# Statistics and attention of a macaron block: normed rows from two tensors, both variances in one addition, maxima turned before the projection

## The chip, the cores and the metric

The kernel runs on one core of a Trainium2 chip. Its time is the device time of one execution in microseconds (us); the number compared is the median of several executions.

## The reference

The input is x of 32 x 256 tokens with 128 features, in fp32. Three steps follow one another, each adding to x:

```
x = x + 0.5 * ffn(layernorm(x))
x = x +       attention(layernorm(x))
x = x + 0.5 * ffn(layernorm(x))

layernorm(x) = (x - mean) / sqrt(var + 1e-5)            over the 128 features
attention:  qkv = x @ (s * W_qkv);  16 heads of 8;  causal softmax(q k^T / sqrt(8)) v;  @ (s' * W_proj)
ffn:        8 experts (128 -> 512 -> 128, gelu), one expert per token by its affinity
            aff = num / (|x| |w|),  num = x @ waff^T;  a token is kept if its rank for its expert is under a capacity
```

The capacity and the ranks need the affinities of all tokens, so each ffn has a routing stage before its experts. s and s' come from spectral norms of the weights.

## The kernel before

The program is a list of blocks in which all engines take part, with a barrier between two: `preamble` (weights, constants), `token_stats` (layernorm statistics and affinity products of the input), `route`, `experts`, `attention`, then `route` and `experts` again. Each engine has its own order of instructions, written out by hand, and waits on semaphores.

**token_stats** goes over 16 batches of 4 tiles of 128 tokens. SP loads a batch (256 KB) into one of four buffers once its former content has been stored. VectorE takes `bn_stats` and `bn_aggr` of each tile, which leaves mean and variance beside the row. Two operations (lines 434 and 435) then put the bare variance and the variance plus 1e-5 into `vare`; POOL raises the two to the powers 0.5 and -0.5 (line 393), which gives the reciprocal deviation for the row and the norm for the affinity. ScalarE's queue stores the rows with their statistics. VectorE norms the tiles of the batch before (line 441, one operation for each of four tiles), PE transposes them and multiplies them with the affinity weights.

**attention** goes over the 32 sequences in turns of 12 steps (u = 0 to 11). A turn b works on several sequences at once. PE's order in each step is: one tile of scores by query of a later sequence, whose row maxima VectorE takes (`tensor_reduce`, line 1341); one tile of scores by key of sequence b (`scores_by_key`, lines 1202 to 1216), which ScalarE turns into exponentials (line 1131) and POOL masks (line 1080); in every third step the products with v; and one small piece of other work (`small`, lines 1236 to 1290). Scores by key alternate between two PSUM banks, so those of step u wait for the exponential of step u - 2; those of step 0 also wait for the maxima, which lie in six rows of `qs`.

The maxima of sequence b + 1 go this way: when VectorE has taken all twelve tiles, POOL splits them into three bf16 pieces in step 5 (lines 1108 to 1114, semaphore `mp_done`); PE transposes them in step 8 into PSUM tile mi[0] (line 1288); ScalarE copies them in step 8, behind the exponential of step 8 (line 1168); SP sends them to `qs` (line 1045); and `scores_by_key` of step 0 of the next turn waits for them (line 1206). In the same step 8, ahead of the transposes, PE multiplies the normalised attention output of sequence b - 1 with W_proj into mi[1] (line 1280, semaphore `proj_mm`), which waits for ScalarE's copy `ont`. VectorE adds the residual in step 9 (line 1376), then takes the statistics of the new rows in steps 10 and 11.

Queries and keys of sequence b + 3 are split into bf16 pieces in steps 2 to 5 (lines 1142, 1350, 1151, and 1102 on POOL), stored to DRAM by SP (line 1040) and loaded back in their final layout, by SP (line 1052) and by ScalarE's queue in steps 9 and 10 (line 1177, three DMAs in each, ahead of the exponential of the next step).

Layernorm appears twice in a turn: for sequence b + 4 before attention (statistics in steps 6 and 7 with one variance, normed rows in step 10), and for sequence b - 2 after it (both variances in step 11, normed rows in step 2 of a later turn). Their helpers are `statistics` (lines 1314 to 1321) and `normalise` (lines 1323 to 1326).

Of the kernel before, what the change touches and what calls it, by code (L numbers as in the profile page):

```python
# [14 lines left out]
ALU = mybir.AluOpType  # L15
# [3 lines left out]
P = 128  # L19
D = 128  # L20
# [3 lines left out]
TPB = S // P  # L24
# [13 lines left out]
LN_EPS = 1e-5  # L38
# [54 lines left out]
def preamble(nc, m, io, c):  # L93

    ctx = ExitStack()
    with ctx:
# [155 lines left out]
        def _(dve):  # L252
            v = nc.vector
# [12 lines left out]
            v.memset(gelu_b1[:, :], 0.0).then_inc(filled, 1)  # L266
            v.memset(c.b1t[:, E, :], 0.0).then_inc(filled, 1)
            v.memset(c.cst[:, :, :], 0.0).then_inc(filled, 1)
            dve.wait_ge(ints, 4)
            for dst, src in ((c.iota[:, :], iota_i[:, :]), (c.part[:, :], part_i[:, :]),  # L270
                             (c.tile1[:, :], tile_i[:, :]), (c.down[:, :], down_i[:, :])):
# [61 lines left out]
def token_stats(nc, m, io, c, x_dram):  # L333
# [3 lines left out]
    with ctx:  # L337
        t = Mem(nc, ctx)
        TS = 4
# [81 lines left out]
        @blk.vector  # L421
        def _(dve):
            v = nc.vector

            def stats(b, k):
                q = k % 2
                dve.wait_ge(x_in[k], b * (16 // NX) + (16 - k * (16 // NX)))
                for j in range(TS):
                    v.bn_stats(bn[:, q, j, :], x_row[k][:, j, 0:D]).then_inc(bn_done, 1)
                dve.wait_ge(bn_done, b * TS + TS)  # L430
                for j in range(TS):
                    v.bn_aggr(x_row[k][:, j, D:D + 2], bn[:, q, j, :]).then_inc(mv_done, 1)
                dve.wait_ge(mv_done, b * TS + TS)
                v.tensor_copy(vare[:, q, :, 1], x_row[k][:, :, D + 1])
                v.tensor_scalar(vare[:, q, :, 0], x_row[k][:, :, D + 1], LN_EPS, None, ALU.add).then_inc(var_done, 1)

            def norm(b, k):
                dve.wait_ge(rstd, b + 1)
                wait(dve, tr, (b - 1) * TS)
                for j in range(TS):  # L440
                    v.tensor_scalar(xn[k % 2][:, j, :], x_row[k][:, j, 0:D], x_row[k][:, j, D:D + 1],
                                    x_row[k][:, j, D + 1:D + 2], ALU.subtract, ALU.mult).then_inc(xn_done, 1)

            def step(b, k, first, last):
                if first:
                    stats(b, k)
                if not last:
                    stats(b + 1, (k + 1) % NX)
                norm(b, k)

            run(step)
# [25 lines left out]
def consts(nc, m):  # L477

    class C:
        pass  # L480
    c = C()
    c.ident, c.ones = m.sb("ident", [P, P]), m.sb("ones", [P, P])
    c.identb, c.onesb, c.tri = (m.sb(n, [P, P], BF16) for n in ("identb", "onesb", "tri"))
    c.tie = m.sb("tie", [P, TPB, S])
    c.mask = m.sb("mask", [P, 4, P], BF16)
    c.iota, c.part, c.tile1, c.down = m.sb("iota", [P, P]), m.sb("part", [P, 1]), m.sb("tile1", [P, NT]), m.sb("down", [P, E])
    c.w1, c.w2 = m.sb("w1", [P, G, F]), m.sb("w2", [P, G, FC, D])


    c.b1t = m.sb("b1t", [P, G, FC])  # L490
    c.cst = m.sb("cst", [P, G, D], BF16)
    c.waff_t, c.wnorm, c.thr = m.sb("waff_t", [P, E]), m.sb("wnorm", [P, E]), m.sb("thr", [P, 1])
    c.wq, c.wk, c.wv, c.wproj = (m.sb(n, [P, D]) for n in ("wq", "wk", "wv", "wproj"))
    c.num, c.xnorm = m.sb("num", [P, NT, E]), m.sb("xnorm", [P, NT])
    c.qs = [m.sb(f"qs{k}", [P, HP, S], BF16) for k in range(NQ)]
    c.kb = [m.sb(f"kb{k}", [P, HP, 2, S], BF16) for k in range(NQ)]
    c.vp = [m.sb(f"vp{k}", [P, TPB, H, 32]) for k in range(NQ)]
    c.gidx, c.sidx = m.sb("gidx", [P, NSX], I32), m.sb("sidx", [P, NSX], I32)
    c.eid = m.sb("eid", [1, NSX], I32)
    c.keep = m.sb("keep", [P, NSX])  # L500
    c.const_parts = m.sb("const_parts", [G, 3, D], BF16)
    c.cst_in = m.sem("cst_in")
    c.place = m.sb("place", [P, NT], I32)
    return c
# [436 lines left out]
def attention(nc, m, io, c, x_dram):  # L941
# [9 lines left out]
    with ctx:  # L951
# [229 lines left out]
        def _(pe):  # L1181
            te = nc.tensor

            def turn(b, k, has):
# [51 lines left out]
                def small(u):  # L1236
                    if u == 0 and has(3):
                        wait(pe, xn_done, (b + 4) * TPB)
                        wait(pe, mt_out, b + 1)
                        wait(pe, v_out, b + 3)  # L1240
                        for j in range(TPB):
                            te.transpose(mi[0][:, j * P:(j + 1) * P], xn[(k + 1) % 2][:, j, :], c.ident[:, :]).then_inc(xt_tr, 1)
                    if u == 3 and has(-2):
                        wait(pe, xn2_done, (b - 1) * TPB)
                        for j in range(TPB):
                            te.transpose(mi[1][:, j * P:(j + 1) * P], xn2[k % 2][:, j, :], c.ident[:, :]).then_inc(x2t_tr, 1)
                    if u == 2 and has(3):
                        wait(pe, xt_out, b + 4)
                        te.matmul(mi[0][:, 0:S], c.wq[:, :], xt[(k + 1) % 2][:, :], start=True, stop=True)
                        te.matmul(mi[0][:, S:2 * S], c.wk[:, :], xt[(k + 1) % 2][:, :], start=True, stop=True).then_inc(qk_mm, 1)  # L1250
                    if u == 7 and has(-2):
                        wait(pe, x2t_out, b - 1)
                        wait(pe, v_out, b + 4, B)
                        for j in range(TPB):
                            last = te.matmul(mi[0][:, j * E:(j + 1) * E], x2t[k % 2][:, j * P:(j + 1) * P], c.waff_t[:, :],
                                             start=True, stop=True)
                        last.then_inc(num_mm, 1)
                    if u == 5 and has(3):
                        wait(pe, r_done, b + 4)
                        for j in range(TPB):  # L1260
                            last = te.matmul(mi[0][:, j * D:(j + 1) * D], xt[(k + 1) % 2][:, j * P:(j + 1) * P], c.wv[:, :],
                                             start=True, stop=True)
                        last.then_inc(v_mm, 1)
                    if u == 5 and has(-1):
                        wait(pe, ot_out, b)
                        wait(pe, x2t_out, b - 1)
                        for j in range(TPB):
                            for half in range(2):
                                at = (2 * j + half) * P
                                last = te.transpose(mi[1][:, at:at + P], ot[(k - 1) % 2][:, half, j * P:(j + 1) * P], c.ident[:, :])  # L1270
                        last.then_inc(otr, 1)
                    if u == 7 and has(-1):
                        wait(pe, on_done, b)
                        for j in range(TPB):
                            last = te.transpose(mi[1][:, j * P:(j + 1) * P], on[(k - 1) % 2][:, j, :], c.ident[:, :])
                        last.then_inc(ont_tr, 1)
                    if u == 8 and has(-1):
                        wait(pe, ont_out, b)
                        for j in range(TPB):
                            last = te.matmul(mi[1][:, j * D:(j + 1) * D], ont[(k - 1) % 2][:, j * P:(j + 1) * P], c.wproj[:, :],  # L1280
                                             start=True, stop=True)
                        last.then_inc(proj_mm, 1)
                    if u == 8 and has(1):
                        wait(pe, mp_done, b + 2)
                        wait(pe, v_out, b + 4, B)
                        wait(pe, num_out, b - 1)
                        for j in range(TPB):
                            last = te.transpose(mi[0].bitcast(BF16)[0:3 * H, j * P:(j + 1) * P],
                                                mp[(k + 1) % 2][:, j, :, :].rearrange("p t h -> p (t h)"), c.identb[:, :])
                        last.then_inc(mt_tr, 1)  # L1290

                for u in range(NP):
                    for o, v in QUERY_TILES[u]:
# [13 lines left out]
        def _(dve):  # L1307
# [6 lines left out]
            def statistics(n, x, bns, var, bnd, mv, done, keep):  # L1314
# [2 lines left out]
                    v.bn_aggr(x[:, j, D:D + 2], bns[:, j, :]).then_inc(mv, 1)  # L1317
                wait(dve, mv, n * TPB + TPB)
                if keep:
                    v.tensor_copy(var[:, :, 1], x[:, :, D + 1])  # L1320
                v.tensor_scalar(var[:, :, 0] if keep else var[:, :], x[:, :, D + 1], LN_EPS, None, ALU.add).then_inc(done, 1)

            def normalise(out, x, done):
                for j in range(TPB):
                    v.tensor_scalar(out[:, j, :], x[:, j, 0:D], x[:, j, D:D + 1], x[:, j, D + 1:D + 2],
                                    ALU.subtract, ALU.mult).then_inc(done, 1)

            def turn(b, k, has):
                for u in range(NP):
# [108 lines left out]
```

## Time and profile before

| | |
|---|---|
| median of 3 runs | 1154.74 us (1152.61 to 1157.74) |
| profiled execution | 1151.91 us, span 1149.8 us |
| PE busy | 910.6 us (79%) |
| VectorE (DVE) busy | 707.3 us (62%) |
| ScalarE (ACT) busy | 592.5 us (52%) |
| GpSimd (POOL) busy | 719.7 us (63%) |
| mean granted TensorE clock | 0.877 of full |

A row of the trace names a line of the kernel, the engine, the operation and the tiles (output, arrow, inputs, buffer numbers left out), and its duration. PE is the matmul, PEld the load of its weights, SPq and ACTq are the queues from which DMAs are issued. In brackets stands how long the engine was idle before the row, and by what the profile supposes that the wait was ended. Where an instruction waits for several semaphores, one releaser is named.

The stages by time: preamble to about 44 us, statistics to 93, the first routing to 165, the experts to 327, attention to 883, the second routing to 950, and the experts to the end.

### The profile page before, as it was taken

The numbers are of one execution on the slowest core, as the hardware profiler recorded it, in microseconds if no ns is written. First come the engines' busy times: TensorE is split into PE (matmuls) and PEld (weight loads), VectorE is DVE, ScalarE is ACT, GpSimd is POOL, SyncE is SP. The second block draws the span as 40 slices with busy tenths as digits, with TensorE's granted clock in tenths as the row PEclk, the third lists the DMA queues.
The fourth block names the chain that finished last, engine by engine and source line by source line (L and its number), as shares of the span: only waits on it lengthen the run. The fifth ranks groups of instructions, "written<-read, shape, count | busy, mean of one in ns | idle before, by whom it ended". The sixth has DMA issues, their size and how long they took to land. (4 is left out here: it accounts for less than half of the span.)

```text
span 1149.8 us, 25202 instructions
## 1 busy us (share of the span) xinstructions
PE 910.6 (79%) x8020; PEld 689.5 (60%) x8054; DVE 707.3 (62%) x2090; ACT 592.5 (52%) x1538; POOL 719.7 (63%) x1170
## 2 busy tenths in 40 slices
PE   2484638999936899999999999999883455988876
PEld 1383218999933566566666666666552225977876
DVE  6587944444416677777778777778654973433332
ACT  3023506666612666666666666666562423654543
POOL 4361976444132677777777777777552596777775
PEclk9655558999968999999999999999996556999998
DMA  5370002222216555555555665555510001212121
GB/s 165 88 191 20 1 9 65 69 67 68 51 47 118 104 104 113 118 117 106 111 108 109 122 116 102 112 113 111 106 27 10 1 1 41 52 52 52 48 50 30
DMA packets 124693, 89.01 MB, mean 77 GB/s; under 512 B 13649, under 2 KB 115078, under 8 KB 124566
## 3 DMA queue, kind: packets, MB, share of 16 engines
q1 hardware_dynamic: 101782, 52.36, 20.8%
q0 software_dynamic: 8960, 18.14, 6.9%
q10 hardware_dynamic: 13824, 16.92, 6.9%
q8 instruction: 68, 1.11, 0.4%
q14 instruction: 59, 0.48, 0.2%
HBM read 52.23 MB, written 34.87 MB: 76 GB/s over the span
## 5 line engine op out<-in xcount | busy, mean ns | idle before, releaser
L1341 DVE TENSOR_REDUCE at_mx<-at_pp 128x2 f32<-128x512 f32 (+1 forms) x384 | 260.4, 687 | 85.9 <-PE at_pp L1199 64.7
L1131 ACT ACTIVATE at_pt<-at_pm 128x512 f32<-128x512 f32 x384 | 224.6, 597 | 143.1 <-PE at_pm L1210 92.7
L1080 POOL TENSOR_SCALAR_AFFINE_SELECT at_pt<-at_pt 128x256 f32<-128x256 f32 (+1 forms) x384 | 182.1, 485 | 127.4 <-ACT at_pt L1131 123.1
L845 ACT ACTIVATE e_ht<-e_ps_h,b1t 128x128 f32<-128x128 f32 x576 | 164.5, 371 | 119.4 <-PE e_ps_h L873 119.2
L807 POOL DMA_INDIRECT e_x<-rows,gidx x144 | 138.6, 963 | 95.0 <-DVE e_y L925 49.1
L873 PE MATMUL e_ps_h<-e_xnt,e_w1own 128*128 128x128 f32 x1152 | 157.8, 281 | 25.5 <-issue 22.0
L873 PEld LDWEIGHTS e_ps_h<-e_xnt,e_w1own 128*128 128x128 f32 x1152 | 143.9, 197 | 29.5 <-issue 28.3
L883 PE MATMUL e_ps_y<-w,e_ht 128*128 x1152 | 160.1, 283 | 0.0
L883 PEld LDWEIGHTS e_ps_y<-w,e_ht 128*128 128x128 f32 x1152 | 140.8, 193 | 1.7
L925 DVE SCALAR_TENSOR_TENSOR e_y<-e_ps_y,e_x 128x256 f32<-128x256 f32 x72 | 30.5, 424 | 143.9 <-PE e_ps_y L883 143.9
L574 POOL TENSOR_SCALAR r_atp<-r_iotab,r_colp 128x128 bf16<-128x128 bf16 x128 | 91.5, 733 | 35.9 <-DVE r_colp L712 35.9
L1231 PE MATMUL at_po<-at_pt,vp 128*32 128x256 f32 (+1 forms) x2048 | 109.8, 332 | 0.9 <-POOL at_pt L1080 0.9
L1210 PE MATMUL at_pm<-qs,kb 128*128 128x256 bf16 x512 | 97.5, 271 | 15.4 <-ACT at_pt L1131 13.5
L1197 PE MATMUL at_pp<-kb,qs 96*128 96x512 bf16 x256 | 98.8, 386 | 2.8 <-DVE at_mx L1341 2.0
L817 POOL DMA_INDIRECT out_dram<-e_y,sidx x72 | 73.4, 1019 | 24.4 <-issue 20.9
L1231 PEld LDWEIGHTS at_po<-at_pt,vp 128*32 128x32 f32 x2048 | 53.4, 109 | 49.7 <-issue 17.6
L1210 PEld LDWEIGHTS at_pm<-qs,kb 128*128 128x128 bf16 x512 | 47.2, 97 | 56.4 <-DMA qs<-at_mt 17.7
L1091 POOL DMA_INDIRECT at_xa<-x,at_index x64 | 63.7, 996 | 13.1 <-issue 10.8
L1199 PE MATMUL at_pp<-mask,identb 128*128 128x256 bf16 x256 | 70.3, 274 | 0.0
L919 DVE COPY e_w1own<-w 128x512 f32 x144 | 63.9, 446 | 8.5 <-issue 7.9
L1192 PE MATMUL at_pp<-kb,qs 96*128 96x256 bf16 x256 | 50.3, 278 | 15.2 <-DMA kb<-at_qkd 14.2
L839 ACT ACTIVATE e_xnt<-e_ps_x 128x256 f32<-128x256 f32 x72 | 27.8, 387 | 52.7 <-PE e_ps_x L866 52.7
(256 smaller groups left out, 1622.7 us busy)
## 6 DMA issues: line engine op xcount, KB each, us to landing
at_qkd<-at_part SPq DMA_DIRECT2D x64, 192.0 KB, 3.0
kb<-at_qkd SPq DMA_DIRECT2D x64, 96.0 KB
qs<-at_qkd ACTq DMA_DIRECT2D x64, 96.0 KB
x<-e_y SPq DMA_DIRECT2D x36, 128.0 KB, 1.8
rows<-ts_x ACTq DMA_DIRECT2D x16, 264.0 KB, 3.1
rows<-at_x SPq DMA_DIRECT2D x32, 132.0 KB
ts_x<-in_x_dram SPq DMA_DIRECT2D x16, 256.0 KB, 3.2
x_by_token<-at_xa SPq DMA_DIRECT2D x32, 128.0 KB
```

The source lines that it names most:

```text
L574: last = g.tensor_scalar(at_p[:, n, :], iotab[:, :], colp[:, n:n + 1], None, ALU.is_equal)
L807: pool.indirect_dma_start(x_row[s][:, j % 2, :], None, rows, bass.IndirectOffsetOnAxis(ap=c.gidx[:, j:j + 1], axis=0)).then_inc(x_in[s], 16)
L817: pool.indirect_dma_start(y_dram, bass.IndirectOffsetOnAxis(ap=c.sidx[:, j:j + 1], axis=0), y_row[s][:, j % 2, :], None, bounds_check=T - ...
L845: last = a.activation(hid_t[j % NB][:, f, :], ps_h[j % NB][:, f, :], ACT.Gelu, bias=c.b1t[:, ds(e, 1), f])
L873: last = te.matmul(ps_h[j % NB][:, f, :], w1_own[j % NB][:, f * P:(f + 1) * P], xn_t[(j // 2) % NX][:, j % 2, :], start=True, stop=True, s ...
L883: last = te.matmul(out, hid_t[j % NB][:, f, :], c.w2[:, ds(e, 1), f, :].rearrange("p a d -> p (a d)"), start=False, stop=(f == FC - 1))
L1080: g.affine_select(out=tile, in_=tile, compare_op=ALU.is_ge, fill=0.0, base=0, pattern=[[0, n], [1, P]], channel_multiplier=-1).then_inc(ma ...
L1131: a.activation(pt[u % RING][:, :], pm[u % 2], ACT.Exp, scale=SCALE).then_inc(exped, 1)
L1197: te.matmul(out, qs[s][0:ROWS, v - 4, P:S], kb[s][0:ROWS, v - 4, :, :].rearrange("p r q -> p (r q)"), start=True, stop=False, skip_group_c ...
L1210: last = te.matmul(out[:, i * S:(i + 1) * S], kb[s][:, g + 2 * w + i, r, 0:P], qs[s][:, g + 2 * w + i, :], start=True, stop=True)
L1231: last = te.matmul(out[32 * j:32 * j + 32, (half + 1) * S - cols:(half + 1) * S], values[:, w // 2, at:at + 32], src[:, i * cols:(i + 1) * ...
L1341: v.tensor_reduce(out, src, axis=AX.X, op=ALU.max).then_inc(maxed, 1)
```

## The change

1. Normed rows, in `token_stats` and in attention's `normalise`: (x - mean) * r was one `tensor_scalar` with two per-partition scalars. It becomes one `scalar_tensor_tensor` with the mean as per-partition scalar and r as a tensor that is one element wide and broadcast over 128.
2. Both variances, in `token_stats` and in `statistics` with `keep`: a `tensor_copy` and a `tensor_scalar` become one `tensor_tensor` addition of the variance, broadcast over two, and a small table `eps` that holds 1e-5 and 0. The single variance becomes a `tensor_tensor` addition with the same table. The table is filled by two `memset`s in the preamble.
3. PE in step 8 of attention: the two transposes of the maxima stand ahead of the projection matmuls, with their waits.

```diff
@@ preamble, VectorE @@
             v.memset(c.cst[:, :, :], 0.0).then_inc(filled, 1)
+            v.memset(c.eps[:, :, 0:1], LN_EPS).then_inc(filled, 1)
+            v.memset(c.eps[:, :, 1:2], 0.0).then_inc(filled, 1)
@@ token_stats, VectorE @@
-                v.tensor_copy(vare[:, q, :, 1], x_row[k][:, :, D + 1])
-                v.tensor_scalar(vare[:, q, :, 0], x_row[k][:, :, D + 1], LN_EPS, None, ALU.add).then_inc(var_done, 1)
+                v.tensor_tensor(vare[:, q, :, :], x_row[k][:, :, D + 1:D + 2].to_broadcast([P, TS, 2]), c.eps[:, 0:TS, :],
+                                ALU.add).then_inc(var_done, 1)
...
-                    v.tensor_scalar(xn[k % 2][:, j, :], x_row[k][:, j, 0:D], x_row[k][:, j, D:D + 1],
-                                    x_row[k][:, j, D + 1:D + 2], ALU.subtract, ALU.mult).then_inc(xn_done, 1)
+                    v.scalar_tensor_tensor(xn[k % 2][:, j, :], x_row[k][:, j, 0:D], x_row[k][:, j, D:D + 1],
+                                           x_row[k][:, j, D + 1:D + 2].to_broadcast([P, D]), ALU.subtract, ALU.mult).then_inc(xn_done, 1)
@@ consts @@
+    c.eps = m.sb("eps", [P, 4, 2])
@@ attention, PE, small(u) @@
-                    if u == 8 and has(-1):
-                        wait(pe, ont_out, b)
-                        ... two projection matmuls, proj_mm
                     if u == 8 and has(1):
                         wait(pe, mp_done, b + 2)
                         wait(pe, v_out, b + 4, B)
                         wait(pe, num_out, b - 1)
                         ... two transposes of mp, mt_tr
+                    if u == 8 and has(-1):
+                        wait(pe, ont_out, b)
+                        ... two projection matmuls, proj_mm
@@ attention, VectorE @@
                 if keep:
-                    v.tensor_copy(var[:, :, 1], x[:, :, D + 1])
-                v.tensor_scalar(var[:, :, 0] if keep else var[:, :], x[:, :, D + 1], LN_EPS, None, ALU.add).then_inc(done, 1)
+                    v.tensor_tensor(var[:, :, :], x[:, :, D + 1:D + 2].to_broadcast([P, TPB, 2]), c.eps[:, 0:TPB, :],
+                                    ALU.add).then_inc(done, 1)
+                else:
+                    v.tensor_tensor(var[:, :], x[:, :, D + 1], c.eps[:, 0:TPB, 0], ALU.add).then_inc(done, 1)
...
-                    v.tensor_scalar(out[:, j, :], x[:, j, 0:D], x[:, j, D:D + 1], x[:, j, D + 1:D + 2],
-                                    ALU.subtract, ALU.mult).then_inc(done, 1)
+                    v.scalar_tensor_tensor(out[:, j, :], x[:, j, 0:D], x[:, j, D:D + 1],
+                                           x[:, j, D + 1:D + 2].to_broadcast([P, D]), ALU.subtract, ALU.mult).then_inc(done, 1)
```

## Rows read from the trace of the kernel before

**Rows 1.** Busy us (times) of each engine, clock, DMA share, GB/s, attention's steady turns

```profile
386.00:851.00 465.00, 439.60 (x4453) 287.25 (x4474) 355.67 (x890) 299.85 (x616) 333.68 (x671) 1.00 0.53 108
```

**Rows 2.** Waits from 400 to 860 us: total, times, longest

```profile
PEld at_pm L1210 <- DMA qs<-at_mt: 17.2, 25, 1.4
```

**Rows 3.** Timeline, parts of one turn: start, duration

```profile
596.32 0.60 ACT L1131 ACTIVATE at_pt<-at_pm 128x512 f32<-128x512 f32 x1 [0.17 <-PE at_pm L1210]
...
596.81 0.59 ACT L1146 ACTIVATE at_ot<-at_po 128x512 f32<-128x512 f32 x1
...
601.43 0.69 PE L1280 MATMUL at_mi<-wproj,at_ont 128*128 128x128 f32 x4
...
601.63 0.60 ACT L1131 ACTIVATE at_pt<-at_pm 128x512 f32<-128x512 f32 x1 [0.28 <-PE at_pm L1214]
...
602.05 0.29 PE L1288 MATMUL at_mi<-identb,at_mp 128*48 128x128 bf16 x2
...
602.38 0.38 ACT L1168 ACTIVATE at_mt<-at_mi 48x256 bf16<-48x256 bf16 x1
...
602.78 0.81 SPq L1045 DMA_DIRECT2D qs<-at_mt  x1
602.81 0.69 DVE L1341 TENSOR_REDUCE at_mx<-at_pp 128x2 f32<-128x512 f32 x1 [0.71 <-PE at_pp L1199]
...
603.93 1.06 ACTq L1177 DMA_DIRECT2D qs<-at_qkd  x3
...
605.09 0.60 ACT L1131 ACTIVATE at_pt<-at_pm 128x512 f32<-128x512 f32 x1 [1.46 <-PE at_pm L1214]
...
605.80 0.13 PEld L1210 LDWEIGHTS at_pm<-qs,kb 128*128 128x128 bf16 x2 [0.69 <-DMA qs<-at_mt]
```

**Rows 4.** Timeline, the same place in another turn

```profile
667.91 0.60 ACT L1131 ACTIVATE at_pt<-at_pm 128x512 f32<-128x512 f32 x1 [1.98 <-PE at_pm L1214]
668.62 0.13 PEld L1210 LDWEIGHTS at_pm<-qs,kb 128*128 128x128 bf16 x2 [1.21 <-issue]
```

**Rows 5.** Timeline, DMA issues of SP and ScalarE in one of five turns

```profile
508.52 0.81 SPq L1045 DMA_DIRECT2D qs<-at_mt  x1
...
509.06 1.82 ACTq L1177 DMA_DIRECT2D qs<-at_qkd  x3
```

**Rows 6.** Timeline, end of the maxima's split and the projection, smallest margin

```profile
584.33 0.24 POOL L1114 TENSOR_TENSOR at_mp<-at_nr,at_mp 128x32 bf16<-128x32 f32 x1
...
584.59 0.69 PE L1280 MATMUL at_mi<-wproj,at_ont 128*128 128x128 f32 x4
```

**Rows 7.** VectorE by line, 0 to 330 us: busy us, mean ns, idle before

```profile
L730 DVE SCALAR_TENSOR_TENSOR r_beats<-r_ps_b,r_amax,tie 128x256 f32<-128x256 f32 x64 | 26.4, 474 | 0.0
...
L441 DVE TENSOR_SCALAR ts_xn<-ts_x 128x128 f32<-128x128 f32 x64 | 17.8, 340 | 1.1 <-POOL ts_x L393 1.1
...
L744 DVE SCALAR_TENSOR_TENSOR r_eidf<-iota,r_tend,r_eidf 128x80 f32<-128x80 f32 x6 | 1.8, 302 | 0.2
```

**Rows 8.** Timeline of the statistics stage

```profile
66.78 0.17 DVE L434 COPY ts_vare<-ts_x 128x4 f32<-128x4 f32 x1
66.86 0.16 DVE L435 TENSOR_SCALAR ts_vare<-ts_x 128x4 f32<-128x4 f32 x1
66.93 1.11 DVE L441 TENSOR_SCALAR ts_xn<-ts_x 128x128 f32<-128x128 f32 x4
...
68.17 1.82 PEld L460 LDWEIGHTS ts_pn<-waff_t,ts_xnt 128*128 128x128 f32 x8
...
70.65 1.81 PEld L460 LDWEIGHTS ts_pn<-waff_t,ts_xnt 128*128 128x128 f32 x8
```

**Rows 9.** Timeline of VectorE in attention's last turns

```profile
868.27 0.60 DVE L1325 TENSOR_SCALAR at_xn<-at_x 128x128 f32<-128x128 f32 x2 [2.69 <-POOL at_x L1096]
```

**Rows 10.** Line 718 in the two routing stages: ns, shortest, median, longest

```profile
L718 DVE TENSOR_TENSOR r_att<-r_ats,r_rank x16: 746/750/753, 122.3 to 938.8; 128x576 bf16<-128x576 bf16 x16
```

**Rows 11.** Timeline of VectorE in the preamble

```profile
33.11 0.28 DVE L308 COPY own_rows<-pre 8x128 f32<-8x128 f32 x1 [6.91 <-PE pre L229]
```

More of the change, by code:

```diff
@@ L1276, in small @@
                         last.then_inc(ont_tr, 1)
-                    if u == 8 and has(-1):
-                        wait(pe, ont_out, b)
[L1279 to L1282, printed above, removed]
                     if u == 8 and has(1):
@@ L1290, in small @@
                         last.then_inc(mt_tr, 1)
+                    if u == 8 and has(-1):
+                        wait(pe, ont_out, b)
+                        for j in range(TPB):
+                            last = te.matmul(mi[1][:, j * D:(j + 1) * D], ont[(k - 1) % 2][:, j * P:(j + 1) * P], c.wproj[:, :],
+                                             start=True, stop=True)
+                        last.then_inc(proj_mm, 1)
                 for u in range(NP):
```

## The prediction

> **What bounds the kernel now.** I read the busy times by stage first. Over attention's steady turns TensorE is busy 439.6 of 465 us at full clock while VectorE has 355.7 [rows 1]: attention is TensorE's, and only what shortens its stalls counts there. The list of waits then names the largest stall that an edit could touch: weight loads of the key scores (line 1210) waiting for "DMA qs<-at_mt", 17.2 us in 25 turns [rows 2]. That is the transfer of the turned maxima, which the change issues earlier, so the label promises a gain. A wait on several semaphores is put down to one of them, however, so I went on to the timeline of one turn [rows 3]. There the first key scores of the next turn need two things: the maxima in qs, and the exponential of step 10, which frees their PSUM bank. That exponential starts at 605.09 and takes 0.60, so it ends at 605.69; the load starts at 605.80, 0.11 later. In all 29 turns whose stall lies between 385 and 828 us the load starts 0.11 or 0.12 us after that exponential's end; one more stands in [rows 4], 668.51 to 668.62, where the same gap carries the label "issue" instead. Only in the first turn of the stage and in its last two is it otherwise. A transfer that landed last would scatter; a constant gap says that the exponential ends the wait and the transfer has landed already. The exponential in turn starts 0.10 us after ScalarE's queue has issued its three loads of qs (603.93 + 1.06 = 604.99 against 605.09), so the chain into the stall is: rest of the split (POOL) to DRAM, its landing, ScalarE's three DMA issues, the exponential, the scores. The maxima are on a side arm of it.
>
> **PE: transposes of the maxima ahead of the projection.** Nothing is added or removed, so PE's own time is the same. Now the four projection matmuls start at 601.43, the two transposes at 602.05, and ScalarE copies them at 602.38 [rows 3]. In the new order the transposes could start at about 601.43 and end 0.29 later, at 601.72. ScalarE is then in the exponential of step 8 (601.63 to 602.23); consecutive ScalarE operations overlap by about 0.1 us (596.32 + 0.60 against a next start at 596.81), so the copy could start at about 602.12, 0.26 earlier, and so could SP's issue (602.78). SP is free: nothing waits in its queue between the split's issues and this one. The copy is followed by the exponential of step 9, which waits for scores that PE reaches at the same time as before. The projection ends 0.29 later, at about 602.41; VectorE reads it in step 9, behind a reduction that itself waits for PE and ends at 603.50, so 1.1 us of cover is left. On the chain above the gain is nothing, since the exponential is what ends the wait.
> There is one side effect that I price. In 5 of the turns ScalarE starts its three DMA issues only 0.54 to 0.68 us after SP has begun to issue the maxima, and there the three take 1.27 to 1.82 us instead of the usual 1.06 (the worst stands in [rows 5], 0.54 us behind SP's issue); they lie on the chain, and exceed 1.06 by 1.9 us in sum. If 0.26 us more distance halves that, the gain is 0.9 us; bounds 0 and 1.9.
> What the new order adds is a wait of the projection, and of all behind it on PE, for the maxima's last piece from POOL. In the turn of [rows 6] POOL ends that piece at 584.57 and PE starts the projection at 584.59: with some 0.06 us for the semaphore this turn would lose about 0.04. In the 28 other turns of that stretch the margin is 0.12 to 0.87 us. Sum under 0.2 us; I take 0.
>
> **VectorE: normed rows by scalar_tensor_tensor.** 64 operations in the statistics stage and 128 in attention change form: one pointer scalar and one broadcast tensor instead of two pointer scalars. The old one takes 340 ns at 128 elements [rows 7]. The new form is in the trace at other sizes: 302 ns at 80 elements, 474 at 256 (that one reads PSUM and writes an accumulator too). On the line between them 128 elements give 302 + 48 x 0.98 = 349 ns, so +9 ns each. Bounds: 302 and 474, that is -38 and +134 ns. I take +9, because 80 elements is the nearer row and it reads SBUF as the new one does. In attention 4 x 9 = 36 ns a turn go into a VectorE that idles 110 of 465 us [rows 1]: nothing. In the statistics stage at most 64 x 9 = 0.6 us, of which I take 0.2, for the reason given next.
>
> **VectorE: one addition for both variances.** 16 copies in the statistics stage and 32 in attention go. In the statistics stage the copy starts at 66.78, the addition at 66.86 and the first normed row at 66.93 [rows 8]: the pair holds the engine for 0.15 us, one operation for about 0.08. I take the new operation to last about as long as the old addition, 0.16 us; then 0.08 a batch go, 1.2 us over 16 batches if all lay on the path. It does not: PE's loads run almost without a gap in this stage, at half clock; its projections repeat every 2.48 us (68.17 to 70.65), which is also VectorE's period, and every fourth batch waits for its load behind the store of the batch that held its buffer. A VectorE that gets 0.08 faster runs into PE at once. I take -0.4, bounds 0 and -1.2, and with the +0.2 above -0.2 for the stage. In attention the variance is 0.08 us earlier for POOL's power, which in the steady turns is reached late anyway. It counts in the last turns only, where VectorE stands 2.69 us waiting for POOL and POOL for it [rows 9]: three such chains, -0.2 us. The single variance of the other rows changes from one operation to one operation: 0.
>
> **The preamble's two memsets** write 4 elements each, fewer than any VectorE operation of [rows 8], which hold the engine for 0.08 us; the chain that they delay ends in a stall of VectorE before line 308 [rows 11], which waits 6.91 us for PE behind the weights. 0; were that cover gone, 0.16 us.
>
> **POOL.** The new operations read two SBUF tensors while POOL's masks and powers run. The row for such a pair in the route stage, with POOL computing on line 574 beside it, is flat: 746 to 753 ns over 16 [rows 10]; VectorE is not stretched. POOL may be. I take 0.
> The Trainium skill ("SBUF — State Buffer", section "SBUF: two separate sides") says that a VectorE operation with two SBUF inputs and a GpSimd operation that reads SBUF exclude each other, the later one blocking; it says the same of a tensor_scalar in a two-port mode, which the old form may be. By that rule the change trades one lock for another and the sum stays; the flat row above shows only VectorE's side of it.
>
> **Sum.** 0 (chain) - 0.9 (DMA issues) - 0.2 (statistics stage) - 0.2 (tail) = -1.3 us on the profiled execution's 1151.9 us, whose span is 1149.8, so 1150.6. That execution is 2.8 us under the median of the three runs shown, 1154.74; from the median I forecast 1153.4 us. The three runs span 5 us, so 0.5% (5.8 us) is about what can be told from no change.
>
> **Rivals.**
> A, the label is right: in most turns the maxima's transfer does land last and the stall shrinks by the 0.26 us by which it is issued earlier. 31 turns x 0.26 = 8 us: 1146.7. For it: the label itself in 25 turns. Against: the constant 0.11 us behind the exponential, and that in [rows 3] SP's issue at 602.78 leaves 3 us before the load. Were it so, it would gain only until the exponential binds. Chance 0.10.
> B, slower by the new wait: POOL comes later than now in step 8 (its mask or its three small steps stretched by VectorE's new form), the transposes wait, and the projection, the scores of step 9 and the exponential wait behind them. It decides where the margin is gone, some 0.13 us in 12 of the 29 turns; with POOL 0.45 us later in all 31, 31 x (0.45 - 0.15) = 9.3 us: 1164. Against: POOL has no new work, and VectorE's form changes outside that step. Chance 0.04.
> C, slower by the port: each normed row waits for the POOL mask beside it, about 0.4 us. Two waits a turn on a reduction that PE waits for make 0.3 us of stall after VectorE's own slack, 31 x 0.3 = 9.3, and in the statistics stage a form of 474 ns would give 64 x 0.134 = 8.6 us on VectorE's path. Either gives about 1163. Against: the flat row [rows 10]. Chance 0.05.
> D, the change does nothing at all, not even on the issues: 1154.7, inside the forecast's own 0.5%.
>
> **Chances.** Forecast with D 0.81, A 0.10, B 0.04, C 0.05. Faster by over 0.5%: A's 0.10, where it is just past the bound, with some of the scatter, 0.10. Slower: 0.08. Same: 0.82. The forecast's own range is 1150 to 1158, scatter of the runs included; for 8 in 10 I reach toward both sides, 1148.5 to 1159.5.
>
> **What would show it.** Right: the transposes (line 1288 now) before the projection's matmuls, ScalarE's copy of them some 0.25 us nearer to step 8's exponential, and yet the load of line 1210 still 0.1 us behind the exponential of step 10, with PE idle there as now, whatever its label. Normed rows of 340 to 355 ns. VectorE's period in the statistics stage 2.4 to 2.5 us. Wrong: loads that start earlier against the scores of step 11 (A), waits of PE on line 1114 by tenths of a us (B), normed rows of 0.4 us and over (C), or a stall that moved to another load, which I could not see from here.

## The result, and the profile after

Median 1161.27 us (1157.14 to 1170.08, 13 runs) against 1155.74 us (1152.61 to 1164.30, 13 runs) of the kernel before on the same chip: 1.0049, with a 95% interval of 1.0026 to 1.0072. The change makes the kernel slower by about half a per cent. The forecast was 1153.4 us with a range up to 1159.5; the time lies outside it.

The profiled execution took 1161.27 us with a span of 1159.3, 9.5 more than before. The page of the kernel after has the same work on every engine as before, within 4 us (PEld had 689.5 before, the others stand above):

```profile
PE 914.1 (79%) x8020; PEld 690.6 (60%) x8054; DVE 709.5 (61%) x2044; ACT 589.1 (51%) x1538; POOL 722.4 (62%) x1170
```

So the time went into waits. I took the start of both routing stages on VectorE (line 671, now 674) and the experts' end as marks. The first routing starts at 96.48 instead of 95.47, attention's first statistics at 332.61 instead of 330.74, the second routing at 893.32 instead of 883.86; behind it both kernels take the same time. Attention thus holds 7.6 of the 9.5 us. Its steady turns (the columns of [rows 1]) now need 472 us for the PE work that 465 held:

```profile
388.00:860.00 472.00, 440.64 (x4443) 287.68 (x4471) 358.40 (x862) 295.52 (x613) 334.95 (x667) 0.99 0.52 106
```

The list of waits of the stretch from 386 to 851 us before (total, times, longest) has these rows for the scores by key and their exponential:

```profile
PEld at_pm L1210 <- DMA qs<-at_mt: 15.9, 24, 1.1
PE at_pm L1210 <- ACT at_pt L1131: 12.3, 21, 2.1
PEld at_pm L1210 <- issue: 7.2, 5, 2.5
ACT at_pt L1131 <- issue: 6.2, 2, 3.2
```

The same view of the kernel after, 388 to 860 us, has these:

```profile
PEld at_pm L1213 <- issue: 27.9, 27, 2.7
ACT at_pt L1134 <- issue: 21.9, 8, 3.5
PE at_pm L1213 <- ACT at_pt L1134: 19.6, 20, 2.4
PEld at_pm L1213 <- DMA qs<-at_mt: 2.5, 3, 1.1
```

Two things are to be seen. The label of the stall in front of PE's loads went over from the maxima's transfer to "issue", and the stall did not get smaller: 15.9 + 7.2 before, 27.9 + 2.5 after, 7.3 us more, which is about attention's loss. And ScalarE's exponential now stands behind its own queue for up to 3.5 us in 8 places instead of 2. The new time is in a few turns. An ordinary turn of the kernel after looks like [rows 3], with the transposes in front (timeline, parts):

```profile
639.06 1.32 SPq L1043 DMA_DIRECT2D at_qkd<-at_part  x2
...
640.32 0.29 PE L1285 MATMUL at_mi<-identb,at_mp 128*48 128x128 bf16 x2
640.54 0.71 PE L1291 MATMUL at_mi<-wproj,at_ont 128*128 128x128 f32 x4
...
640.92 0.36 ACT L1171 ACTIVATE at_mt<-at_mi 48x256 bf16<-48x256 bf16 x1
...
642.69 4.32 SPq L1055 DMA_DIRECT2D kb<-at_qkd  x6
642.75 1.06 ACTq L1180 DMA_DIRECT2D qs<-at_qkd  x3
...
643.91 0.60 ACT L1134 ACTIVATE at_pt<-at_pm 128x512 f32<-128x512 f32 x1 [1.47 <-PE at_pm L1217]
...
644.62 0.13 PEld L1213 LDWEIGHTS at_pm<-qs,kb 128*128 128x128 bf16 x2 [0.70 <-issue]
```

The next but one looks like this:

```profile
670.06 1.32 SPq L1043 DMA_DIRECT2D at_qkd<-at_part  x2
...
675.07 4.32 SPq L1055 DMA_DIRECT2D kb<-at_qkd  x6
675.40 1.39 ACTq L1180 DMA_DIRECT2D qs<-at_qkd  x3
676.89 0.60 ACT L1134 ACTIVATE at_pt<-at_pm 128x512 f32<-128x512 f32 x1 [3.46 <-issue]
...
677.61 0.13 PEld L1213 LDWEIGHTS at_pm<-qs,kb 128*128 128x128 bf16 x2 [2.69 <-issue]
```

The loads of SP and ScalarE wait for the store of the split. They come 3.63 us behind its first issue in the one (639.06 to 642.69) and 5.01 us in the other (670.06 to 675.07), and the load of PE is again 0.1 us behind the exponential's end. I call this distance the store's landing, and a landing over 4.4 us late. Of the 29 turns that have both scores by key and a store of the split (numbered from 0), 2 are late before and 6 after. Timed from the exponential of step 4 to the same one of the next turn, a late turn takes 17.8 us on the mean and the others 15.6, in both kernels: 2.2 us each.

What lies beside a late store is seen in the DMA view of a window of 6 us around it. In the window of the ordinary turn, 639 to 645 us, there is no packet of queue q8 (the last number of the row is the median of us to landing, of the two DMAs):

```profile
at_qkd<-at_part SPq DMA_DIRECT2D x2, 192.0 KB, 3.0
```

The late one, 669.5 to 675.5 us:

```profile
q8 instruction: 1, 0.02, 1.0%
...
at_qkd<-at_part SPq DMA_DIRECT2D x2, 192.0 KB, 3.7
```

The page counts 68 such packets of instructions, 1.11 MB in all, so 16 KB each. I take q8 as PE's stream: it is the longest, as PE's 8020 + 8054 records are the most (some 240 to a packet), and instructions added to PE alone move its packets (h1, below). That it is PE's is inferred, since no row names the engine.

The same view shows what is late about the store. Each of its two DMAs ends with 16 packets of 4 bytes, the writes of its semaphore. In the first 3.5 us of the ordinary store (639.06 to 642.56) all 32 are there, the packets under 512 bytes; in those of the late one (670.06 to 673.56) 31:

```profile
DMA packets 800, 0.39 MB, mean 112 GB/s; under 512 B 32, under 2 KB 800, under 8 KB 800
```

```profile
DMA packets 776, 0.40 MB, mean 114 GB/s; under 512 B 31, under 2 KB 775, under 8 KB 775
```

Without q8's packet the late store has 775, so 25 are missing: one write and 24 of the 768 data packets of 512 bytes, a sixteenth of the second half. They follow up to 4.6 us. So one share of sixteen is held up while the others are on time. In the profiles of all sixteen unsplit kernels below it is the same in every late store whose packet lies 2.3 us or more behind the issue: at most two of the 32 writes come after 3.5 us, the last at 4.3 to 5.0.

### The profile page after: what moved, and what is told of

The parts are those of the page before. It is cut to its first block and busy times, and to the rows that moved or that the text cites. A ratio compares the mean times of both kernels' runs of the same rounds, so it can differ in the third digit from the quotient of the medians.

```text
span 1159.3 us, 25156 instructions
## 1 busy us (share of the span) xinstructions
PE 914.1 (79%) x8020; PEld 690.6 (60%) x8054; DVE 709.5 (61%) x2044; ACT 589.1 (51%) x1538; POOL 722.4 (62%) x1170
## 3 DMA queue, kind: packets, MB, share of 16 engines
q8 instruction: 68, 1.11, 0.4%
```

## The experiments

All on one core, in four sessions on four chips, each against the kernel before in the same session. Its median was 1155.7 us in the session of h and k and 1155.8 us in that of p, and 1222.9 and 1217.9 us in those of e and g (mean granted clock 0.85 to 0.87 there against 0.87 to 0.88); ratios are taken inside a session. The chips of h, k and p, which run the kernel as fast as that of the result, are called the first kind. Late stores are counted in one profiled execution of each kernel.

### The parts alone

**e1_reorder**, **e2_norm**, **e3_var**, **e4_vector_only**: on the kernel before, the PE order alone; the two normed-row edits alone; the variances alone; all VectorE edits without the PE order. Each is its part of the diff shown above.

> Only the order on PE is changed in step 8: transposes of the maxima ahead of the projection. Theory S (stores land late): the maxima's transfer is issued 0.26 us earlier, into the tail of the split's store, which in five or six turns, instead of two, lands 5.0 to 5.6 us after its issue rather than 3.6, where PE's instruction fetch falls into it; each such turn costs about 1.5 us. S expects most of the loss here: 4 to 6 us slower than before. Theory V (the vector forms cost it: normed rows that exclude POOL's reads and lengthen the statistics stage): within 1 us of before. Theory F (only the phase of an instruction stream against the turns, which any edit shifts): anything from -4 to +5 us, and not additive with the other edits.

> Only the normed rows become scalar_tensor_tensor, in the statistics stage and in attention. S: +1 us (the statistics stage, which was 1 us later in the changed kernel's profile), attention unchanged. V: +4 to +6 us, with normed rows of step 2 at 437 ns instead of 346 and stalls behind them. F: -4 to +5.

> Only the variances become one addition with the table (and the two memsets). 48 instructions fewer on VectorE. S and V: -0.5 to +0.3 us. F: -4 to +5, since VectorE's instruction stream is shorter.

> Both vector edits, PE's order as before. S: +0.5 to +1.5 us against before. V: +4 to +6, as much as the whole change. F: not the sum of the two runs with one vector edit each.

Measured: 1.0006 [0.9978, 1.0033], 0.9948 [0.9918, 0.9978], 1.0020 [0.9990, 1.0049], 0.9950 [0.9923, 0.9977]. Only the runs with the normed rows stand out, and as a gain, though the whole change was slower on the first chip. So the whole and two of the parts were run in a further session, on a chip of the slower kind.

**g1_after**, **g3_reorder**, **g4_norm** are the changed kernel, e1 and e2 once more. **g2_late** is the changed kernel with SP made to send the maxima later:

```diff
                     wait(sp, mt_out, b + 2)
+                    wait(sp, main_done, b * NP + 10)
```

> The changed kernel itself, beside the runs below. If this chip is like the first: 1.003 to 1.007 of before; if it is like that of the four runs before this one (before at 1223 us): the sum of its parts there, 0.5% faster to no change.

> The changed kernel, with SP waiting for the scores of step 9 before it issues the maxima's transfer, so that it starts some 0.3 us later than in the kernel before instead of 0.26 us earlier. Theory S (the earlier transfer runs into the tail of the split's store and makes more stores land late): the loss goes, 2 to 6 us faster than the changed kernel, with two or three late stores instead of six. Theory F (phases of PE's instruction fetches against the turns) and V (vector forms): as the changed kernel, within 2 us.

> The order on PE alone, again, for another chip. S: slower than before by about as much as the whole change on a chip where that is slower. F and V: no more than 1 us from before, as on the other chip (1.0006).

> The normed rows alone, again. S: +1 us. V: on a chip where the whole change is slower, as slow as it. F: as on the other chip, where it was 0.5% faster (0.9948), or anything else within 0.5% of before: the same edit with another sign from chip to chip would speak for F.

Measured: 1.0018 [0.9993, 1.0042], 0.9986 [0.9957, 1.0014], 1.0022 [0.9993, 1.0051], 0.9983 [0.9957, 1.0009]. The gain of the normed rows was 0.5% in one session and 0.2%, with 1 inside, in the next: no effect that I could build on. g2 sends the maxima 2.8 us behind the store's issue (median) instead of 2.25, and has 7 late stores, as against 6 in g1; a later transfer of the maxima does not take them away. Its median is 2.8 us under that of g1, which theory S had forecast together with two or three late stores; with 12 runs of each, no difference is inside the interval, so the time decides nothing here.

### Other places for the instruction packets

**h1_pad64** is the kernel before, **h3_after_pad64** the changed one, each with 64 small matmuls in the preamble, where PE waits for weights. They shift all later PE instructions by 128, half a packet.

```diff
             pe.wait_ge(b1_g, 1)
+            for _ in range(64):
+                nc.tensor.matmul(pm[7][:, 0:1], c.identb[:, :], c.identb[:, 0:1], start=True, stop=True, skip_group_check=True)
             pe.wait_ge(w_ffn, 32)
```

> The kernel before with 64 one-column matmuls (128 instructions with their weight loads) put on PE in the preamble, where PE waits for the weights of the experts; their result is not used. Nothing changes in attention but where PE's instruction fetches fall. Theory F (a store of the split lands late in those turns in which PE's instruction packet falls 2.5 to 3.6 us behind its issue): the late stores, in turns 4, 9, 14, 18, 19 and 28 in all kernels so far, move to other turns, about half a period of 4.7 turns away; the number may change by two or three, and the time by 3 us either way. S and V say nothing that would move them: the same turns, and before's time within 1 us.

> The changed kernel with the same 64 matmuls. F: late stores in the same turns as in the padded kernel before, and a distance between the two padded kernels that differs from the one between the unpadded. S and V: as much slower than the padded kernel before as the change is (0.2 to 0.5%).

Measured: 0.9971 [0.9944, 0.9998] and 1.0040 [1.0015, 1.0065]. The late stores moved to other turns: 10, 11, 20, 25 in h1 and 6, 10, 11, 15, 20, 24, 25 in h3, where the unpadded kernels have theirs in 3, 4, 8, 13, 17, 18, 22 and 27 (numbered from 0; the expectations number them from 1). The work of those turns is the same in all; what moved with the padding is the packet.

### The store's landing taken off the chain

**k1_split** (on the kernel before) and **k2_split_after** (on the changed one) give each half of the split's store a semaphore of its own, so that ScalarE's first three loads and SP's wait for the first half alone. No work is left out.

```diff
-        part_out = [sem(f"part_out{k}") for k in range(2)]
+        part_out = [[sem(f"part_out{r}{k}") for k in range(2)] for r in range(2)]
...
-                                     part[h][64 * r:64 * r + 64, :, :]).then_inc(part_out[h], 16)
+                                     part[h][64 * r:64 * r + 64, :, :]).then_inc(part_out[r][h], 16)
...
-                    wait(sp, part_out[h], dma_count(n, 2, 2)(h))
                     for r in range(2):
+                        wait(sp, part_out[r][h], dma_count(n, 2)(h))
```

(and the same in ScalarE's queue)

> The kernel before, with one semaphore for each half of the split's store, so that the three loads of step 9 on ScalarE's queue (and SP's first three) wait for the first half alone, which is all they read. If the chain named in the prediction is what ends each turn (store's landing, ScalarE's DMA issues, exponential of step 10, scores of step 0), ScalarE's issues start up to 0.6 us earlier, bounded by the exponential of step 9, and PE's stall at line 1210 shrinks from about 0.7 us to 0.2: 8 to 16 us faster, and the late stores cost half. If something else bounds the turn (the maxima's transfer, as the label of the waits says): no change within 2 us.

> The same on top of the changed kernel. If the chain is as said: 8 to 16 us faster than the changed kernel. Here the earlier transfer of the maxima, by 0.26 us, could count for the first time, since it may be the next thing that ends the wait: up to 4 us faster than the split kernel before; if it never binds, the two split kernels are equal.

Measured, against 1155.65 us: k1 **1140.84 us**, 0.9868 [0.9830, 0.9906], and k2 1140.71 us, 0.9869 [0.9832, 0.9906]. Both are 1.3% faster than the kernel before, and the whole change costs nothing on top. By the measure used above, SP's first load, which now waits for the first half of the store alone, no turn is late in either. The turn of k1 that has a packet at the worst place, 2.8 us behind the store's issue (timeline, parts):

```profile
440.12 1.32 SPq L1040 DMA_DIRECT2D at_qkd<-at_part  x2
...
443.45 4.32 SPq L1052 DMA_DIRECT2D kb<-at_qkd  x6
443.51 1.06 ACTq L1178 DMA_DIRECT2D qs<-at_qkd  x3
...
444.67 0.60 ACT L1131 ACTIVATE at_pt<-at_pm 128x512 f32<-128x512 f32 x1 [1.33 <-PE at_pm L1211]
...
445.38 0.13 PEld L1211 LDWEIGHTS at_pm<-qs,kb 128*128 128x128 bf16 x2 [0.56 <-DMA qs<-at_mt]
```

The packet is there (DMA view, 440 to 446 us of k1), and the whole store is as slow as in a late turn, but SP's and ScalarE's loads start 3.33 and 3.39 us behind its issue:

```profile
q8 instruction: 1, 0.02, 1.0%
...
at_qkd<-at_part SPq DMA_DIRECT2D x2, 192.0 KB, 3.9
```

In the busy times of k1's steady turns PE holds 445.3 of 465 us where it held 439.6 [rows 1], and the row "exponential behind issue", 6.2 us with a longest of 3.2 before, has a longest of 0.8:

```profile
382.00:847.00 465.00, 445.31 (x4513) 289.28 (x4539) 363.75 (x902) 304.69 (x623) 337.04 (x677) 1.00 0.50 109
```

```profile
ACT at_pt L1131 <- issue: 6.0, 8, 0.8
PE at_pm L1211 <- DMA qs<-at_mt: 4.7, 8, 1.2
```

The second row has no counterpart in the list of the kernel before. In k1 the load of line 1211 no longer starts 0.11 us behind the exponential in every turn: in 8 of the 29 it starts 0.5 to 1.6 us behind it and waits for the maxima. Once the store's landing is off the chain, the side arm is the next thing that ends the wait in these turns. With the maxima sent earlier (k2) it does so in 3 turns, yet the two medians are equal within 0.3%; what k2 loses elsewhere is open.

### The parts again, plain and padded

**p1_reorder** and **p2_vector** are e1 and e4 on the first kind of chip, **p3_pad_reorder** and **p4_pad_vector** the same two with the 64 matmuls.

> The order on PE alone, meant for a chip like the first, on which the change costs 0.5% (0.7% with the padding). Theory R (the order on PE lets PE's fetch and the earlier transfer of the maxima meet the end of the store more often): 1.003 to 1.007. Theory N (the vector forms push VectorE and POOL, and with them the store, later against PE): 0.998 to 1.001. Theory F (no part owns it; each binary has its own number of late stores): neither, and not additive.

> Both vector edits, PE's order as before. R: 0.997 to 1.001. N: 1.003 to 1.007. F: anything in 0.995 to 1.005.

> The order on PE alone, with the 64 matmuls in the preamble; to be held against the padded kernel before (0.9971 of before) and the padded changed kernel (1.004). R: 1.002 to 1.006, near the padded changed kernel. N: 0.995 to 0.999, near the padded kernel before. F: no relation to the unpadded run of the same edit.

> Both vector edits with the 64 matmuls. R: 0.995 to 0.999. N: 1.002 to 1.006. F: no relation to the unpadded run of the same edits.

Measured: 1.0033 [1.0004, 1.0061], 1.0007 [0.9974, 1.0040], 1.0016 [0.9987, 1.0045], 1.0042 [1.0010, 1.0074]. Plain, only the PE order's loss is clear of noise, though the two intervals overlap. Padded the loss is not the order's alone: against h1's 0.9971 (another session) the order costs 0.45% and the VectorE edits 0.71%, and together (h3) they cost 0.69%. The times of single kernels do not add up. Theory N's range came true for p4 and theory R's nearly for p3, which no single one of the parts explains; that is nearest to theory F. The count below does not explain p4's median either: p4's profiled execution has 1 late store and took 1151.5 us, 8.7 us under the median of its 12 runs. One profile does not give the usual count of its kernel.

### All sixteen unsplit profiles together

They are profiles of eleven kernels, six with the old order and five with the new one: g1 is the changed kernel again, g3 and p1 are e1, g4 is e2, p2 is e4. The counts do separate the orders. Packets are told by their distance to the store's issue:

| eight profiles each | late stores of 29 | packets 2.3 to 3.1 us behind the store, and late | 3.1 to 3.75 us, and late |
|---|---|---|---|
| old PE order (before, e2, e3, e4, g4, h1, p2, p4) | 2, 5, 4, 3, 6, 4, 3, 1: mean 3.5 | 5, of these 4 | 66, of these 23 |
| new PE order (after, e1, g1, g2, g3, h3, p1, p3) | 6, 6, 6, 7, 6, 7, 6, 5: mean 6.1 | 30, of these 28 | 48, of these 19 |

Of 77 late stores 74 have a packet in one of these two columns, the other three one at 0.6 us; no turn without a packet is late. A packet at 2.3 to 3.1 us makes the store late in 32 of 35 cases, one at 3.1 to 3.75 us in 42 of 114. With the old order a profile has 0 or 1 of the early kind, with the new one 2 to 5: no overlap. And 2.6 late stores more, at 2.2 us each, are 5.7 us; the medians of after and before differ by 5.5. The agreement is partly luck. On the first kind of chip alone it is 3.5 stores more, which would be 7.7 us, while the mean ratios of the two orders differ by 0.3%, 3.4 us; on the other kind 1.8 more, 3.9 us, against 0.3%, 4.0 us. So the price holds within a factor of about two.

In the profiled executions of the first kind of chip the time goes roughly with the count; h1 stands above its place, 10 us over its own median:

| kernel | k1 | k2 | p4 | before | p2 | h1 | p3 | p1 | after | h3 |
|---|---|---|---|---|---|---|---|---|---|---|
| late stores | 0 | 0 | 1 | 2 | 3 | 4 | 5 | 6 | 6 | 7 |
| us of that execution | 1142.4 | 1143.0 | 1151.5 | 1151.9 | 1154.8 | 1162.8 | 1161.3 | 1159.6 | 1161.3 | 1166.7 |

## Why the prediction was wrong

**The chain was named rightly.** The forecast put the stall on the store of the split, its landing, ScalarE's three DMA issues and the exponential of step 10, with the maxima on a side arm. The load of line 1213 still stands 0.11 or 0.12 us behind that exponential in all 29 turns, and splitting the store's semaphore moved the kernel by 15 us. The label "DMA qs<-at_mt" [rows 2] was indeed false: after the change the same wait, not shorter, is called "issue". Rival A is refuted.

**The step that failed** is the first term of the sum, "On the chain above the gain is nothing", 0 us. It held for the typical turn. But it took the landing of the store for a fixed length, since it was read from the turn of [rows 3], and priced the new order by the instructions that it moves alone. The landing had two values before already: the profile of before holds two turns of 16.9 and 18.8 us beside 27 of 15.6, and the "issue" row with 2 waits of up to 3.2 us. The forecast looked only at what each turn has in common. With the new order PE's instruction packets fall more often 2.3 to 3.1 us behind the store, and 2.6 more turns of 29 become late: some +5.7 us for a term of 0. Shown are the packet beside each late store, the late turns that move with the padding, the count by PE order, and that the loss is gone when the landing is off the chain. Not shown is that the count gives the whole loss: padded, the VectorE edits without the new order are as slow (p4). Nor is shown why the new order moves the packets. PE's stream is as long as before, and the order differs only inside step 8. g2 had 2 packets of the early kind, the fewest of the eight, so the maxima's transfer may take part; it was not tested by itself.

**The side effect** was priced at -0.9. Over the 29 turns ScalarE's three issues exceeded their 1.06 us by 3.9 us in 12 turns before and by 2.4 us in 6 turns after. Of these, 2.6 us in 8 turns before and 0.7 us in one after belong to issues that start less than 0.9 us behind SP's issue of the maxima; the forecast had counted 5 such turns with 1.9 us. The gain came, 1.5 us in all and 1.9 by the nearer turns, more than the 0.9 forecast, and is lost in the rest.

**Reorder, local steps.** As forecast: copy of the maxima 0.26 us nearer to step 8's exponential, projection 0.3 later and covered. Rival B did not come: the transposes wait for the maxima's last piece from POOL in one turn, 0.2 us.

**Normed rows.** Forecast 349 ns. VectorE by line over 0 to 95 us of the kernel after (busy us, mean ns, idle before), and over 389 to 868:

```profile
L443 DVE SCALAR_TENSOR_TENSOR ts_xn<-ts_x 128x128 f32<-128x128 f32 x64 | 18.2, 346 | 1.2 <-POOL ts_x L395 1.2
```

```profile
L1330 DVE SCALAR_TENSOR_TENSOR at_xn<-at_x 128x128 f32<-128x128 f32 x60 | 24.2, 442 | 10.1 <-POOL at_x L1099 9.9
L1330 DVE SCALAR_TENSOR_TENSOR at_xn<-at_xa 128x128 f32<-128x128 f32 x54 | 16.3, 343 | 0.0
```

Before, the middle one was:

```profile
L1325 DVE TENSOR_SCALAR at_xn<-at_x 128x128 f32<-128x128 f32 x60 | 20.9, 390 | 11.2 <-POOL at_x L1096 11.1
```

346 and 343 ns where nothing is beside it; 442 instead of 390 in step 2, where POOL starts a mask at the same time (the form before took 339 ns with nothing beside it):

```profile
522.83 0.79 DVE L1330 SCALAR_TENSOR_TENSOR at_xn<-at_x 128x128 f32<-128x128 f32 x2 [0.25 <-POOL at_x L1099]
...
523.02 1.09 POOL L1083 TENSOR_SCALAR_AFFINE_SELECT at_pt<-at_pt 128x256 f32<-128x256 f32 x2
```

The two masks that run beside it take 0.45 and 0.68 us where they took 0.42 and 0.63. This is rival C's mechanism at a tenth of a microsecond a turn, in an engine with slack: p2, which has it without the new PE order, is at 1.0007. The flat row of the routing stage [rows 10] did not stand for this pair of operations. The Trainium skill ("SBUF — State Buffer", section "SBUF: two separate sides") has a VectorE operation with two SBUF inputs and a GpSimd operation that reads SBUF exclude each other. The rise from 390 to 442 ns here leans that way, but the rows of both engines overlap in time, and a lock held for the whole of a mask (0.41 us and more) would cost more than the row shows.

**Statistics stage.** Forecast -0.2 us. The period fell to 2.45 us (forecast 2.4 to 2.5, before 2.49):

```profile
67.52 0.17 DVE L436 TENSOR_TENSOR ts_vare<-ts_x,eps 128x8 f32<-128x8 f32 x1
...
69.97 0.17 DVE L436 TENSOR_TENSOR ts_vare<-ts_x,eps 128x8 f32<-128x8 f32 x1
```

Yet this execution reached the routing 1.0 us later. Over the profiles of the first kind of chip the mark is at 96.5, 94.9, 95.7, 95.1 and 94.4 with the new form (after, k2, h3, p2, p4) and at 95.5, 95.4, 95.6, 97.7 and 97.4 with the old (before, k1, h1, p1, p3). That scatter is larger than the term, and the +1.0 lies within it; -0.2 is neither confirmed nor refuted.

**Base and range.** The profile of before had 2 late stores where profiles with the old order have 3.5 on the mean, and was 3.8 us under the median of 13 runs: the reading started from a lucky execution. The forecast took its base from the median of the three runs instead, which was only 1.0 us low. The chance of 0.08 for slower had no case for "the same chain, longer in some turns".

## What to carry to other kernels

Where a stage has a steady turn, list the length of every turn before reading one: the few long turns of the kernel before already showed which wait varies and what it costs, and a chance price on it belongs in the sum. An edit that only reorders one engine's instructions can move when its instruction packets cross a critical transfer. The cure is to give the transfer slack rather than to look for a lucky order: one semaphore for each half of the store was worth 1.3%, more than any part of this change gave on any chip (0.5% at best).

## What the runs showed of the hardware

A single 16 KB packet of instructions, taken to be PE's, was beside every late landing of a 384 KB store: 3.6 us becomes 4.5 to 5.6 us. The late store of the changed kernel at 670.06 us landed 1.4 us later than the ordinary one; the packet itself took 1.0 us of one DMA engine (1.0% of sixteen engines over 6 us). One sixteenth of the store's second half was held up, and the loads wait for all of it. A packet at 3.1 to 3.75 us did so in 42 of 114 cases, one at 2.3 to 3.1 us in 32 of 35. The kernel's scatter is smaller without the wait: on one chip before ran from 1149.6 to 1162.5 us over 23 runs (standard deviation 3.8), k1 from 1137.3 to 1143.3 over 6 (2.0) and k2 from 1139.2 to 1143.1 over 6 (1.6). That the late stores make the difference is likely but not shown, since one execution of each kernel was traced.

The stall's label changed from a transfer to "issue" with the maxima's transfer 0.26 us earlier, while the load stayed 0.11 us behind the exponential in all 29 turns before and after.
